# Softplus step size summed on TensorE, its product taken on VectorE, and the second channel half prepared one batch later

## What is computed

```
xz = x @ W_x.T;  dt_raw, B, C = xz[..., :128], xz[..., 128:144], xz[..., 144:160]
dt  = softplus(dt_raw @ W_dt.T + b_dt)            # [8, 512, 512]
d_a = exp(dt[..., None] * -exp(A_log))            # 16 states for each channel
dbx = dt[..., None] * B[:, :, None, :] * x[..., None]
h_t = d_a_t * h_{t-1} + dbx_t                     # along the 512 rows of a batch
y_t = sum over the 16 states of h_t * C_t;  out = y + x * D_param
```

## Time and profile before

| | us |
|---|---|
| runs | 3055.64, 3056.68, 3058.74 (median 3056.68) |
| the profiled execution's span, first to last instruction | 3057.4 |
| scan stage, first to last scan instruction | 36.4 to 1047.1 |
| busy in these 1010.7 us: POOL / DVE / PE / ACT | 973.2 / 965.3 / 843.2 / 654.0 |
| experts, attention, experts again | 1047.1 to 3057.4 |

### The profile page before, as it was taken

The page is one execution under the profiler, slowest core; times in us unless marked ns, Lnnn a source line. Parts: engine busy times, 40 slices in busy tenths (PEclk is TensorE's granted clock), DMA queues, the critical chain, the costliest instruction groups (busy, mean ns, idle before and its releaser), DMA issues.

```text
span 3057.4 us, 37567 instructions
## 1 busy us (share of the span) xinstructions
PE 2742.0 (90%) x13484; PEld 1445.2 (47%) x13484; DVE 1789.4 (59%) x3787; ACT 1298.1 (42%) x2689; POOL 1529.0 (50%) x944
## 2 busy tenths in 40 slices
PE   4668889898998879988868999999899999999998
PEld 2455555555555534333325555555544444444443
DVE  5899999999999742222236666665624444222222
ACT  4557576675866411110107666766722220111111
POOL 6999999999999702212125555555500001121211
PEclk7769999998998989989979999999999999999999
DMA  5344544545545479999960000000225323999997
GB/s 194 141 167 153 195 172 161 192 155 182 180 167 174 141 273 352 340 336 341 336 201 1 29 29 29 29 29 15 89 87 181 121 86 130 312 334 336 342 348 219
DMA packets 198955, 557.76 MB, mean 182 GB/s; under 512 B 24880, under 2 KB 26800, under 8 KB 198256
## 3 DMA queue, kind: packets, MB, share of 16 engines
q1 hardware_dynamic: 180624, 513.27, 48.7%
q0 software_dynamic: 17088, 40.90, 5.8%
q10 hardware_dynamic: 1056, 1.18, 0.1%
HBM read 479.50 MB, written 75.79 MB: 182 GB/s over the span
## 4 chain that ended last, share of the span: by engine, by line
PE 54%; DVE 3%; ACT 2%; POOL 2%; issue 2%; DMA 1%; POOLq 0%; SPq 0%; DVEq 0%; ACTq 0%
PE bank L1133 11%; PE bank L1159 5%; PE bank L1036 5%; PE bank L1057 5%; PE bank L1071 5%; PE bank L1184 5%; PE bank L1241 4%; PE bank L1218 3%; PE bank L1206 2%; PE bank L1230 2%; POOL arena L1940 2%; PE bank L1116 1%; PE bank L1172 1%; ACT arena L1763 1%; PE bank L1043 1%
## 5 line engine op out<-in xcount | busy, mean ns | idle before, releaser
L1844 POOL TENSOR_TENSOR arena<-arena 128x1024 f32<-128x1024 f32 x256 | 607.5, 2373 | 7.9 <-PE bank L986 5.0
L1692 ACT ACTIVATE bank<-arena 128x512 f32<-128x512 f32 x512 | 346.6, 689 | 317.6 <-DVE arena L1330 198.5
L986 PE MATMUL bank<-arena 128*128 128x128 f32 x2048 | 306.3, 303 | 146.1 <-POOL arena L1850 145.8
L1940 POOL TENSOR_TENSOR arena<-arena 128x2048 f32<-128x2048 f32 (+3 forms) x128 | 296.9, 2323 | 276.4 <-DVE arena L1560 276.3
L986 PEld LDWEIGHTS bank<-arena 128*128 128x128 f32 x2048 | 260.4, 156 | 231.7 <-POOL arena L1850 186.2
L1763 ACT ACTIVATE arena<-arena 128x256 f32<-128x256 f32 (+3 forms) x512 | 287.3, 566 | 148.8 <-DVE arena L1551 125.2
L1133 PE MATMUL bank<-arena 128*64 128x352 f32 x2048 | 343.1, 491 | 0.0
L1850 POOL TENSOR_TENSOR arena<-arena 128x512 f32<-128x512 f32 x256 | 333.8, 1304 | 17.5 <-DVE arena L1330 17.5
L1330 DVE TENSOR_TENSOR_SCAN arena<-bank,arena 128x512 f32<-128x512 f32 x256 | 310.7, 1214 | 26.5 <-POOL arena L1844 19.4
L1330 DVE TENSOR_TENSOR_SCAN bank<-bank,arena 128x512 f32<-128x512 f32 x256 | 308.4, 1205 | 0.0
L1057 PE MATMUL bank<-arena 128*128 128x512 f32 x640 | 288.3, 593 | 7.6 <-ACT arena L1719 7.6
(11 more groups left out here) (145 smaller groups left out, 4159.0 us busy)
## 6 DMA issues: line engine op xcount, KB each, us to landing
arena<-scratch_bc SPq DMA_DIRECT2D x128, 1024.0 KB, 5.4
arena<-in_w_gate SPq DMA_DIRECT2D x128, 704.0 KB
arena<-in_w_up SPq DMA_DIRECT2D x128, 704.0 KB
arena<-in_w_down SPq DMA_DIRECT2D x128, 512.0 KB
arena<-in_w_down SPq DMA_DIRECT2D x128, 192.0 KB
scratch_x<-arena SPq DMA_DIRECT2D x16, 1024.0 KB, 4.5
scratch_xn<-arena SPq DMA_DIRECT2D x15, 1024.0 KB, 4.1
arena<-scratch_x SPq DMA_DIRECT2D x44, 256.0 KB, 6.0
```

The lines of the kernel that those rows point to most:

```text
L986: i = nc.tensor.matmul(y[:, t * P:(t + 1) * P], w[:, n, t * P:(t + 1) * P], p.ident, is_transpose=True, start=False, stop=g == GROUPS - 1 ...
L1692: nc.scalar.activation(bank[p.da_bank(k, n)][:, :], block_of(p.dt, b, c), ACT.Exp, scale=p.alog[:, c, state:state + 1]).then_inc(*p.decaye ...
L1844: nc.gpsimd.tensor_tensor(out=p.hb[k % HB], in0=over(block_of(p.dtx, b, c), 1, NG), in1=p.bc[k // 2 % NBC][:, 0], op=ALU.mult).then_inc(*p ...
L1940: nc.gpsimd.tensor_tensor(out=own, in0=own, in1=over(p.rden[:, k % 2, :], 2, width), op=ALU.mult).then_inc(*p.divided.up(k))
```

## The change

The sum of the two softplus parts moves from VectorE to TensorE: two matmuls with the identity add the two SBUF tiles of one block into a bank. ScalarE copies the bank into the `dt` tile, and VectorE multiplies the same bank with x and writes `dtx`, where GpSimd did it before. All three work on single blocks (128x512) in place of halves (128x1024). The two `dt` products of blocks 2 and 3, their softplus, sum and product move from steps 22 to 31 of the batch before into steps 1 to 10 of the batch itself (33 to 42 in the tables). `dt` of blocks 0 and 1 goes from step 21 to 19. Four of the six gate/up pairs of the shared expert start earlier.

```diff
-TURN_S, DTR, BC, DT = (13, 13, 14, 14), 16, 15, (21, 21, 22, 25)
-SOFT = (("soft_exp", (24, 28)), ("soft_ln", (26, 29)), ("dt_sum", (27, 30)), ("dtx", (28, 31)))
+TURN_S, DTR, BC, DT = (13, 13, 14, 14), 16, 15, (19, 19, 33, 34)
+SOFT = (("soft_exp", (22, 36)), ("soft_ln", (24, 37)))
+DSUM, COPY_LAG, DTX_LAG = (26, 27, 39, 40), 1, 2
...
-GATES, UPS = (23, 26, 29, 30, 32, 35), (23, 26, 29, 30, 33, 35)
+GATES, UPS = (20, 23, 25, 29, 32, 35), (20, 23, 25, 29, 33, 35)
...
+        yield DSUM[c], ("dsum", b, c)
+        yield DSUM[c] + COPY_LAG, ("dt_copy", b, c)
+        yield DSUM[c] + DTX_LAG, ("dtx", b, c)
...
-TAKERS = ("turned", "dtr_out", "bc_out", "dt_out", "logit", "folded", "silu", "hid", "so")
+TAKERS = ("turned", "dtr_out", "bc_out", "dt_out", "dt_copy", "dtx", "logit", "folded", "silu", "hid", "so")
...
+    def dt_sum(b, c):
+        ring = p.rings[0]
+        out = bank[ring.bank("dsum", b, c)]
+        PE.wait_bank(ring, "dsum", b, c)
+        PE.wait_ge(p.soft_ln, b, c // 2)
+        nc.tensor.matmul(out[:, :], p.ident, block_of(p.dt, b, c), start=True, stop=False)
+        nc.tensor.matmul(out[:, :], p.ident, block_of(p.dtx, b, c), start=False, stop=True).then_inc(
+            *ring.made.up("dsum", b, c))
...
-    def dt_sum(b, h):
-        V.wait_ge(p.soft_ln, b, h)
-        dt, soft = half_of(p.dt, b, h), half_of(p.dtx, b, h)
-        nc.vector.tensor_tensor(out=dt, in0=dt, in1=soft, op=ALU.add).then_inc(*p.dt_ready.up(b, h))
+    def dtx(b, c):
+        ring = p.rings[0]
+        V.wait_ge(ring.made, "dsum", b, c)
+        V.wait_ge(p.dt_ready, b, c)
+        nc.vector.tensor_tensor(out=block_of(p.dtx, b, c), in0=bank[ring.bank("dsum", b, c)][:, :],
+                                in1=p.s_xnT[b % 2][:, c, :], op=ALU.mult).then_inc(
+                                    *ring.taken_by["dve"].up("dsum", b, c))
...
+    def dt_copy(b, c):
+        ring = p.rings[0]
+        A.wait_ge(ring.made, "dsum", b, c)
+        nc.scalar.copy(block_of(p.dt, b, c), bank[ring.bank("dsum", b, c)][:, :]).then_inc(*p.dt_ready.up(b, c))
...
-    def dtx(b, h):
-        xnT = p.s_xnT[b % 2][:, h * (HC // 2):(h + 1) * (HC // 2), :]
-        G.wait_ge(p.dt_ready, b, h)
-        nc.gpsimd.tensor_tensor(out=half_of(p.dtx, b, h), in0=half_of(p.dt, b, h), in1=xnT,
-                                op=ALU.mult).then_inc(*p.dtx_ready.up(b, h))
```

More of the change, by code:

```diff
@@ L807, in semaphores @@
         self.soft_exp, self.soft_ln = sig("soft_exp", "soft_exp"), sig("soft_ln", "soft_ln")
[L808 removed]
+        self.dt_ready = sig("dt_ready", "dt_copy")
         self.bc_in = [sig(f"bc_in{r}", "bc_in", by=16, where=lambda n, r=r: n % NBC == r) for r in range(NBC)]
@@ L1243, in attn_out @@
         i.then_inc(*ring.made.up("wo", b, t))
-    work = {"constants": constants, "barrier": barrier, "turn": turn, "bc": bc, "dtr": dtr, "dt": dt, "sum": y_sum,
+    work = {"constants": constants, "barrier": barrier, "turn": turn, "bc": bc, "dtr": dtr, "dt": dt, "dsum": dt_sum, "sum": y_sum,
             "gate": gate, "gate_wide": gate_wide, "sg": shared_gate, "su": shared_up, "sd": shared_down, "fold": fold, "merge": merge,
@@ L1581, in vector_engine @@
     work = {"constants": constants, "barrier": barrier, "stats": stats, "stats_a": stats_a, "apply": apply, "decay_w": decay_w,
-            "dt_sum": dt_sum, "scan": scan, "x1": x1, "hid": hidden, "so": shared_out,
+            "dtx": dtx, "scan": scan, "x1": x1, "hid": hidden, "so": shared_out,
             "route_max": route_max, "route1": route1, "masks": masks, "folded": folded, "pick": pick, "merge": merge, "lists": lists,
@@ L1941, in divide @@
                                 op=ALU.mult).then_inc(*p.divided.up(k))
-    work = {"constants": constants, "barrier": barrier, "sums": sums, "rstd": rstd, "dtx": dtx, "feed": feed, "weigh_c": weigh_c, "route_w": route_w,
+    work = {"constants": constants, "barrier": barrier, "sums": sums, "rstd": rstd, "feed": feed, "weigh_c": weigh_c, "route_w": route_w,
             "so": shared_sum, "turnover": turnover, "gather": gather, "give": give,
```

20 lines of the change are left out of this document (12 added, 8 removed).

## The result

The changed kernel takes **3094.14 us** (median of 4 runs, 3091.66 to 3097.85) against 3057.71 (4 runs, 3055.64 to 3060.85) for the kernel before in the same comparison: a ratio of **1.0128, 95% interval 1.0107 to 1.0148**, slower by 36 us. The prediction said 3049, with a range up to 3075. The profiled execution has a span of 3096.0 us.

A forecast was written before the change was run, and what follows sets the result against it. The prediction took GpSimd, VectorE and TensorE, running in step in the scan stage, as the bound. 3057.4 - 59.3 of gains + 52.3 of TensorE cost gave 3050.4, with the clock 3048.9, said as 3049 us; range 3022 to 3075.

The forecast's parts named there:

- (a): GpSimd's queue in the scan stage: 15 `dtx` products of 2.32 us go, a gain of 34.8 us.
- (b): GpSimd's waits for VectorE's scan go with `dt_sum`, a gain of 17.5 us.
- (c): GpSimd's seven stretched weighings, one a batch, each lose 1.0 us of stretching: a gain of 7.0 us.
- ScalarE pays 32 copies of 0.59 ..., hidden: ScalarE in the scan stage: 19 us of copies, hidden beside 357 us of idle time, so no cost.
- Moving `dt` of blocks 2 and 3 to steps 1 and 2 costs nothing: TensorE at steps 1 and 2: less busy there, so no cost; without that cover 1.7 us a batch.
- the start-up: Before the scans: identity matmuls, copy and product of one block replace the first `dtx`; counted as nothing.
- The cost on TensorE: Identity sums of 1.74 us in TensorE's queue make later sums and GpSimd's feeds late: 52.3 us in all.
- the prediction's term for step 20: Gate/up pair behind the down product waits for VectorE; feed of step 24 late by 5.4 us, 4.8 in batches 3 and 5.
- The clock: TensorE's granted clock in odd batches: a busier TensorE may keep it up, 0.5 us gained in each of three.
- Rival 1: TensorE's sums don't come late in a way that counts, GpSimd alone paces: 2998 us, chance 0.15.
- rival 2: The early bound at step 20: VectorE keeps close to GpSimd, wait 3.4 in place of 5.4 us: 3037 us, chance 0.12.
- Rival 3: Step 20's pair waits for a late VectorE, each lateness feeding the next: 9.2 us a batch, 3072 us, chance 0.18.

The follow-up runs named there:

- f1: The changed kernel with ScalarE's copy of each sum one step later in the lists, nothing else moved: 3070.8 us, 1.0046 of the kernel before.
- f6: The changed kernel without ScalarE's copies, so the decays lack a term of the step size: 3072.0 us, 1.0047 of the kernel before.
- g1: f1 with the first gate/up pair at step 21 in place of 20: 3065.8 us, 1.0040 of the kernel before.
- g5: g3 with exp and ln of the second half back at steps 4 and 5: 3049.7 us, 0.9987 of the kernel before.
- g3: g1 with `dt` of blocks 2 and 3 at step 31, exp and ln sooner (steps 2 and 4): 3047.7 us, 0.9975 of the kernel before.
- g6: g3 with the first gate/up pair back at step 20: 3062.4 us, 1.0018 of the kernel before.
- h4: g3 with one matmul in each identity sum in place of two, the other term left out: 3038.5 us, 0.9956 of the kernel before.
- e2: The changed kernel with the second half of the step size made in the batch before, as it was: 3080.3 us, 1.0095 of the kernel before.
- e4: The kernel before with only the change of places, VectorE adding and GpSimd multiplying as before: 3099.3 us, 1.0147 of the kernel before.
- g2: g1 with the second half in the batch before, identity sums at steps 30 and 31: 3059.9 us, 1.0022 of the kernel before.
- g4: The kernel before with only the change of engines, places as before, and the copy a step later: 3089.3 us, 1.0119 of the kernel before.
- e1: The changed kernel with the gate/up pairs back at their old steps, first at 23: 3115.0 us, 1.0207 of the kernel before.

## Why the prediction was wrong

**The gains were right.** (a) `dtx` is gone from GpSimd. (b) Its wait for the scan went from 17.5 us to nothing. (c) The mean weighing fell by 26 ns, 6.7 us over 256, for 7.0 predicted. VectorE's product takes 0.68 us and ScalarE's copy 0.59.

**The failed steps were two that the prediction set at zero.** The first is "ScalarE pays 32 copies of 0.59 ..., hidden". The cover was 357 us of idle time, but a copy is not only its 0.59 us. It waits for TensorE, and ScalarE runs its items in the order of the list, so the decays wait with it. f1 prices this at 0.8%, 25 us, and f6 prices the copy's own work at nothing. The prediction looked at what stands behind a waiting instruction in TensorE's queue and not in ScalarE's.

The second is "Moving `dt` of blocks 2 and 3 to steps 1 and 2 costs nothing", with TensorE's lower load as cover. The products' time is 1.7 us a batch; what they cost was the ring. With the first pair at 21, g1 to g5 prices that at 0.53%, 16 us, and with the sooner `ln` (g3) it is 20. With the pair at 20, where the change has it, the same move with the sooner `ln` is f1 to g6: 0.28%, 9 us.

So with both steps set right and every other place as in the change the kernel is g6, at 1.0018: 34 of the 45 us between 3094 and 3049 are accounted for. The remaining 11 us (14 by g6's ratio) are a third error, which the runs don't break down. About 3 us of them stand at the start-up, which the prediction counted as nothing too: the first scan starts at 39.7 us in g6's profiled execution, 36.4 before. Moving the pair to 21 gives 13 us more (g3), but that takes away a stand that the prediction had priced, so it doesn't repair the sum; that g3 comes out at about 3049 is luck.

**The cost on TensorE was of the right kind.** An identity sum takes 1.72 us at full clock (532.88 - 531.16 in the changed kernel) for 1.74 predicted. In batch 4 the feeds wait 1.04 + 2.71 us at steps 12 and 13 (2.3 predicted) and 1.42 + 6.08 at steps 23 and 24 (5.4). With the two forgotten waits gone, all waits of feeds for sums are 63.4 us in g6, which still has the stand at step 20, and 56.9 in g3; the prediction had 52.3 on top of 5.0. But a feed's wait is not a loss of that size: taking away half of TensorE's new work (h4) gave 6 us, taking the pair from 20 to 21 gave 13 (g6 to g3) where the prediction's term for step 20 was 3 x 5.4 + 2 x 4.8 = 25.8. The other waits of a batch absorb part. In the bounds of this term the prediction counted six batches, where its own sum and the traces have five; its 3037 and 3072 would have been 3039 and 3068.

**The clock.** The prediction took 1.5 us off because a busier TensorE would keep the clock up in the odd batches. It rose there, from 0.93 to 0.97 in batches 3 and 5, and in the whole stage from 0.89 to 0.92. In batch 4 it fell from 0.99 to 0.96, where the new stand of 6 us ahead of the narrow pair is followed by half the clock. The sign was right for the batches that it was meant for; what it was worth no run shows.

**The rivals.** Rival 1 (sums never late) is refuted by the feeds' 74.7 us, and rival 2, which had 3.4 us for the wait at step 24, by its 6.08. The rule that went with rival 1, the Trainium skill (Perfetto Trace Analysis, "Identifying the Most-Contended Engine"), to judge TensorE's headroom by its weight loads, is borne out as far as load goes: they are 71 of 136 us in batch 4 of the changed kernel, and h4 shows half of the identity sums' matmuls worth 6 us. It says nothing of when a result is ready, which decided here. Rival 3's mechanism was there (TensorE waits 9.7 us for L1389 in five batches) and not its 9.2 us a batch; the 6.08 us come mostly from what stands in front.

**What stays open.** The rest of that third error, and the sizes of e2, e4, g2 and g4, which no single wait explains. The terms are not additive: the move of the pairs to step 20 gains 0.8% with the copy early (e1 to the change); between 20 and 21 nothing is gained with `dt` at steps 1 and 2 (f1, g1), yet 0.43% with `dt` at 31 (g6, g3). The trace of g1 has one cause for the second: its step 22 falls to 4.4 us as it should, but step 10 of its batches 4 and 6 takes 8.8 and 10.9 us, 5.4 in f1, at half clock (last section). That is the fastest of its ten runs, so it doesn't tell what the median lost.

## What to carry to other kernels

Before calling an operation hidden under idle time, ask what it waits for and what stands behind it in its engine's queue: the 0.59 us copy cost 25 us by its place and nothing by its length. Where products rotate through a few banks, an item added anywhere shifts the bank of every later one; list for each product which taker frees its bank and at what step, and keep that a step or two ahead. A change of engines and a change of places should be tried apart and together: each alone lost here (1.0239, 1.0147), and together with three places mended (the copy, `dt`, the first pair) they beat the kernel before (0.9975).
